# Turning h and the similarity's rows by transposing DMAs in a four-layer graph kernel, with four adjacency buffers

## Chip, cores and metric

One core of a Trainium2 chip. The metric is the device time of one execution in microseconds (us), median over runs.

## What is computed

Four pre-normalised graph layers with a residual each, on x (4096 x 256) and a dense adjacency A (4096 x 4096), all float32:

```python
h = relu(layernorm(x)); x = x + relu(An @ (A2 @ h @ W.T))         # A2 = A + I, An = d * A2 * d
h = relu(layernorm(x)); g = h @ Wg                                  # attention layer
x = x + softmax(cos(g, g) + log(A + 1e-8)) @ g + bias               # cos: rows of g scaled to length 1
h = relu(layernorm(x)); x = x + relu((dn * A * dn) @ h @ W2 + b2)   # dn from A's row sums
h = relu(layernorm(x)); t = relu([h, A @ h] @ W1)
x = x + relu([t, A @ t] @ W2')
```

## The kernel before, in words

**Passes.** The adjacency is gone through six times, passes 0 to 5: 0 and 1 are the first layer, 2 (`ATT`) is attention, 3 the third layer, 4 (`TURNED`, its result transposed) and 5 the fourth. A pass has 8 groups (`NG`) of 512 result rows, and a group has 8 chunks (`NC`) of 512 adjacency rows, 1 MB each. For float32 accuracy every operand is split into two float16 halves: ACT writes the upper half `ahi` of a chunk (`split`, L789), DVE the lower half `alo` (L1036), and PE multiplies upper by upper, upper by lower and lower by upper with the moving rows `mov` (`product`, L472 to L477; `product_turned`, L483 to L485). A chunk is 4 row blocks b of 4 products. Passes 1, 3 and 5 make a product from one 512-column and one 256-column matmul, passes 0 and 2 from three of 257, 256 and 257 columns, where the odd column gives row sums. `adj`, `ahi` and `alo` have two buffers each: SP loads chunk c when DVE has split chunk c-2 (`load`, L314), and ACT splits chunk c when PE has left chunk c-2 (`chunk_done`).

**The tail of a group.** While PE multiplies group g, the results of group g-1 go through stages: `ev` (out of PSUM), `epi`, `x` (residual), `stats` and `norm` of the layer norm, `h` (relu and its halves in `hsp`, ACT L868, DVE L1147), then the turn of h: PE transposes `hsp` block by block into `psT` (L547, stages T0 and T1, 8 transposes each), ACT copies it to `hT` (`keep_hT`, L879), and PE multiplies `hT` by the next weights (`small`, W0 and W1, 12 matmuls of 256 columns each, 24 in pass 3's tail, L592 to L594), whose result is split into `mov` (L901, L1171). In pass 1's tail the result is also scaled to unit rows (`n0`, `n1`: ACT L913, DVE L1185), turned by PE (`G0`, `G1`, `turn_gn`) and kept in `gnT` (L918) for the similarity (`cosines`, L701 to L703). Before pass 0 the same stages turn the first h (tail `PRE`).

**Order.** Each engine runs its own program in order, and tables by hand (`PLACES`, `ATT_PLACES`) say behind which chunk, and on PE behind which (chunk, block), each stage stands. PE: `(3, 3): T0, (4, 0): W0T1, (5, 0): W1, (6, 0): G0, (6, 2): G1` (L626). ACT: L946, DVE: L1218; there a stage at c stands behind split c. POOL (`tail`, L423) computes `own`, the group's own rows for the identity in A2 (L431, as soon as `mov` is there), and the powers -1/2 (`rstd` L417, `rowp`, `rnorm` L442). ACT's and SP's DMAs have a queue each; before the change ACT issues two, at the start.

Of the kernel before, what the change touches and what calls it, by code (L numbers as in the profile page):

```python
# [60 lines left out]

WARM = [60, 60]
# [9 lines left out]
def build(nc, x, adj_t, w0, wg, bias_g, w2, bias_2, w3a, w3b, sent, out):  # L72
# [4 lines left out]
    with ctx:  # L77
# [14 lines left out]
        gnT = shared[:, :].bitcast(f16).rearrange("p (q n) -> p q n", q=2 * FB)  # L92
# [54 lines left out]
        psT = pb("psT", [P, 2 * FB, 2 * P], f16)  # L147
# [3 lines left out]
        psT2 = psS[:, 0, :].bitcast(f16).rearrange("p (q n) -> p q n", q=2 * FB)  # L151
# [7 lines left out]
        adj_loaded = [sem(f"adj_loaded{s}") for s in range(2)]  # L159
# [42 lines left out]
        hT_ready = sem("hT_ready")  # L202
# [9 lines left out]
        gn_turned = sem("gn_turned")  # L212
        gnT_ready = sem("gnT_ready")
# [4 lines left out]
        NORM = [PRE, 1, 2, 3]  # L218
        SMALL = [PRE, 1, 2, 3, 4]
# [41 lines left out]
        def exp_slot_free(eng, g, H):  # L261

            g, H = (g, H - 4) if H >= 4 else (g - 1, H - 4 + NH)
            if g < 0:
                return
# [22 lines left out]
        def small_bank(p, b):  # L288

            if p == TURNED:  # L290
                return psW[:, :] if b % 2 == 0 else psS[:, 0, :]
            bank = psS[:, 0, :] if p == 3 else psS[:, 1, :] if p == PRE and b >= 2 else psW
            return bank[:, (b % 2) * F:(b % 2 + 1) * F]
# [5 lines left out]
        def _(sp):  # L299
# [36 lines left out]
            def group(p, g, first=False):  # L336
                for c in range(2 if first else 0, NC):
                    load(p, g, c)
# [16 lines left out]
            def att_half(g, H):  # L355

                c = H // 2
                if g == 0 and H < 4:
                    sp.wait_ge(split_ready, chunk_no(ATT - 1, NG - 1, NC - 2 + c) + 1)
# [44 lines left out]
        def _(pool):  # L404
# [18 lines left out]
            def tail(p, g):  # L423
                if p in SELF:
# [37 lines left out]
        def _(pe):  # L462
            def product(p, g, c, b, k, first, last):
# [10 lines left out]
                n = F + 1  # L474
# [47 lines left out]
            def turn(p, g, r):  # L522


                pe.wait_ge(h_ready, at(SMALL, p, g))

                if p == PRE:

                    if g > 0:
                        pe.wait_ge(hT_ready, at(SMALL, p, g - 1, 2, r + 1))  # L530
                elif r == 1:
                    pe.wait_ge(hT_ready, at(SMALL, p, g, 2, 1))
                elif not isinstance(g, int) or g > 0:
                    pe.wait_ge(hT_ready, at(SMALL, p, g - 1, 2, 2))
                    if p == 1:
                        pe.wait_ge(gnT_ready, at([1], p, g - 1, 2, 2))
                else:
                    before = SMALL[SMALL.index(p) - 1]
                    pe.wait_ge(hT_ready, at(SMALL, before, NG - 1, 2, 2))
                    if p == 2:  # L540
                        pe.wait_ge(gnT_ready, at([1], 1, NG - 1, 2, 2))
                transposes(r, work(p, g)[1], psT2 if p == PRE and r == 1 else psT).then_inc(h_turned, 1)

            def transposes(r, hsp, to):
                for q in range(2 * FB):
                    for b in range(2):
                        last = nc.tensor.transpose(to[:, q, b * P:(b + 1) * P],  # L547
                                                   hsp[:, q // FB, 2 * r + b, (q % FB) * P:(q % FB + 1) * P],
                                                   ident[:, :])
                return last  # L550

            def small(p, g, r):

                whi, wlo = weights_of[p]
                if p == TURNED:

                    pe.wait_ge(h_ready, at(SMALL, p, g))
                else:

                    pe.wait_ge(hT_ready, at(SMALL, p, g, 2, r + 1))  # L560

                if p == PRE:

                    if g > 0:
                        pe.wait_ge(mov_ready, at(MOVE, p, g - 1, GB, 2 * r + 2))
                elif r == 1:
                    pe.wait_ge(mov_ready, at(MOVE, p, g, GB, 2))
                    if p == 1:
# [789 lines left out]
```

## Time and profile before

| | |
|---|---|
| median of 3 runs | 2486.02 us (2483.68 to 2486.75) |
| span of the profiled execution, the only time that it has | 2484.0 us |
| busy: PE, PE's weight loads, DVE, ACT, POOL | 98%, 66%, 59%, 46%, 6% |
| DMA | 473 MB, 191 GB/s on average |
| passes, us from the start | 0: 82 (start before it), 1: 407, 2: 777, 3: 1370, 4: 1787, 5: 2140 |

An engine's busy time says how much of the span it had an instruction in work. Matmuls overlap in the pipe, so PE's true pace is read from one start to the next. A wait "PE acc L472 <- DVE alo L1036: 12.1, 8, 1.7" says that PE sat idle 12.1 us in 8 times, at most 1.7, until DVE's L1036 had written `alo`.

### The profile page before, as it was taken

Reading aid. Unit: us, or ns where it says so; the run is one execution under the profiler, and the core shown is the slowest. Engines: PE = TensorE matmul, PEld = TensorE weight load, DVE = VectorE, ACT = ScalarE, POOL = GpSimd, SP = SyncE. Lnnn points to the kernel's source line nnn. Section 1 sums busy time; section 2 is a strip of 40 time slices with the busy share of each in tenths; the row PEclk is TensorE's granted clock in tenths of the full one; section 3 lists DMA queues with packets and bytes.
Section 4 is the critical chain, followed back from the end, with each engine's and each line's share of the span. In section 5 each row is a group of like instructions: output and inputs, shape, how many; then the busy total and the mean of one; then the engine's idle time right before and its main releaser. Section 6 shows DMA issues by size and latency. Waiting matters only on the chain.

```text
span 2484.0 us, 43195 instructions
## 1 busy us (share of the span) xinstructions
PE 2434.0 (98%) x17096; PEld 1640.3 (66%) x17096; DVE 1462.1 (59%) x1899; ACT 1145.1 (46%) x1435; POOL 143.5 (6%) x114
## 2 busy tenths in 40 slices
PE   7999999999999999999999999999999999999999
PEld 6888887656666767777888666666544444555555
DVE  7655555666666566666777665566544444455555
ACT  6544443555555544444444444444434334343433
POOL 2300000111110000000000010001000000000000
PEclk9999999999999999999999999999999999999999
DMA  5455555545454766676676544444455455456564
GB/s 204 154 202 188 201 195 194 187 169 178 176 178 158 205 181 201 213 244 206 217 241 231 187 170 169 169 171 167 169 180 186 175 179 184 177 198 219 209 218 170
DMA packets 113727, 473.23 MB, mean 191 GB/s; under 512 B 14432, under 2 KB 47456, under 8 KB 72672
## 3 DMA queue, kind: packets, MB, share of 16 engines
q1 hardware_dynamic: 113344, 471.13, 55.5%
q8 instruction: 65, 1.06, 0.2%
q10 hardware_dynamic: 288, 0.79, 0.1%
q14 instruction: 30, 0.25, 0.0%
HBM read 438.32 MB, written 33.55 MB: 190 GB/s over the span
## 4 chain that ended last, share of the span: by engine, by line
issue 66%; PE 26%; POOL 5%; DMA 1%; DVE 1%; ACT 1%; POOLq 0%; SPq 0%; ACTq 0%; DVEq 0%
PE acc L472 8%; PE acc L483 4%; PE acc L485 4%; PE acc L484 4%; PE acc L473 4%; POOL rstd L417 3%; POOL own L431 1%; DMA adj<-in_adj_t 1%; DVE alo L1036 1%; ACT ahi L789 1%; PE psS L594 0%; PE psS L592 0%; PE psS L593 0%; POOL d L450 0%; PE psW L592 0%
## 5 line engine op out<-in xcount | busy, mean ns | idle before, releaser
L1036 DVE SCALAR_TENSOR_TENSOR alo<-adj,ahi 128x2048 f16<-128x2048 f32 x320 | 743.5, 2323 | 683.0 <-ACT ahi L789 683.0
L472 PE MATMUL acc<-mov,ahi 128*128 128x512 f16 x3072 | 1002.4, 379 | 26.4 <-DVE alo L1036 26.4
L789 ACT ACTIVATE ahi<-adj 128x2048 f16<-128x2048 f32 x320 | 610.9, 1909 | 716.9 <-PE acc L473 337.5
L473 PE MATMUL acc<-mov,alo 128*128 128x256 f16 x3072 | 837.3, 273 | 0.0
L475 PE MATMUL acc<-mov,ahi 128*128 128x257 f16 x2048 | 558.1, 273 | 4.3 <-DVE alo L1036 2.4
L476 PE MATMUL acc<-mov,ahi 128*128 128x256 f16 x2048 | 560.9, 274 | 0.0
L477 PE MATMUL acc<-mov,alo 128*128 128x257 f16 x2048 | 556.2, 272 | 0.0
L472 PEld LDWEIGHTS acc<-mov,ahi 128*128 128x128 f16 x3072 | 300.5, 98 | 386.6 <-DVE alo L1036 32.0
L473 PEld LDWEIGHTS acc<-mov,alo 128*128 128x128 f16 x3072 | 300.6, 98 | 34.5
L475 PEld LDWEIGHTS acc<-mov,ahi 128*128 128x128 f16 x2048 | 196.8, 96 | 46.2 <-DVE alo L1036 4.4
L476 PEld LDWEIGHTS acc<-mov,ahi 128*128 128x128 f16 x2048 | 197.9, 97 | 39.4
L477 PEld LDWEIGHTS acc<-mov,alo 128*128 128x128 f16 x2048 | 202.0, 99 | 26.6
L981 ACT ACTIVATE ahi<-nums 128x512 f16<-128x512 f32 x256 | 160.5, 627 | 100.0 <-DVE nums L1248 98.9
L483 PE MATMUL acc<-ahi,mov 128*128 128x512 f16 x512 | 194.1, 379 | 1.5 <-DVE alo L1036 1.5
L484 PE MATMUL acc<-alo,mov 128*128 128x512 f16 x512 | 194.0, 379 | 0.0
L485 PE MATMUL acc<-ahi,mov 128*128 128x512 f16 x512 | 194.0, 379 | 0.0
L1248 DVE SCALAR_TENSOR_TENSOR nums<-adj,expo 128x512 f32<-128x512 f32 (+2 forms) x144 | 93.1, 646 | 153.3 <-ACT expo L964 153.1
L964 ACT ACTIVATE expo<-psS 128x512 f32<-128x512 f32 (+2 forms) x144 | 81.0, 562 | 209.9 <-PE psS L703 185.0
L1255 DVE SCALAR_TENSOR_TENSOR alo<-nums,ahi 128x512 f16<-128x512 f32 x256 | 175.3, 685 | 0.1
L417 POOL TENSOR_TENSOR rstd<-vare,neghalf 128x4 f32<-128x4 f32 x32 | 77.3, 2414 | 1184.5 <-DVE vare L1126 1184.5
L1248 DVE SCALAR_TENSOR_TENSOR nums<-adj,psS 128x512 f32<-128x512 f32 (+2 forms) x136 | 86.7, 637 | 36.2 <-PE psS L688 22.3
L701 PE MATMUL psS<-shared 128*128 128x512 f16 (+3 forms) x288 | 103.5, 361 | 0.4 <-DVE nums L1248 0.4
(109 smaller groups left out, 1965.3 us busy)
## 6 DMA issues: line engine op xcount, KB each, us to landing
adj<-in_adj_t SPq DMA_DIRECT2D x320, 1024.0 KB, 4.8
adj<-in_adj_t SPq DMA_DIRECT2D x128, 512.0 KB, 4.8
sent<-expo SPq DMA_DIRECT2D x112, 256.0 KB, 2.8
expo<-sent SPq DMA_DIRECT2D x56, 512.0 KB, 5.1
xres<-in_x SPq DMA_DIRECT2D x7, 512.0 KB, 9.9
out<-xres SPq DMA_DIRECT2D x7, 512.0 KB, 6.5
xres<-in_x ACTq DMA_DIRECT2D x1, 512.0 KB, 3.3
shared<-in_w3a SPq DMA_DIRECT2D x1, 512.0 KB, 6.5
```

Of the source, the lines that this page charges most:

```text
L472: nc.tensor.matmul(acc[:, b, :].rearrange("p (s n) -> p s n", s=2), hi, both, start=first, stop=False)
L473: return nc.tensor.matmul(acc[:, b, 0:F], lo, m[:, jb, 0:F], start=False, stop=last)
L475: nc.tensor.matmul(acc[:, b, 0:n], hi, m[:, jb, 0:n], start=first, stop=False)
L476: nc.tensor.matmul(acc[:, b, 0:F], hi, m[:, jb, LO:LO + F], start=False, stop=False)
L477: return nc.tensor.matmul(acc[:, b, 0:n], lo, m[:, jb, 0:n], start=False, stop=last)
L483: nc.tensor.matmul(acc[:, f, :], hi, ahi[:, c % 2, k, :], start=first, stop=False)
L484: nc.tensor.matmul(acc[:, f, :], hi, alo[:, c % 2, k, :], start=False, stop=False)
L485: return nc.tensor.matmul(acc[:, f, :], lo, ahi[:, c % 2, k, :], start=False, stop=last)
L789: nc.scalar.activation(ahi[:, c % 2, :, :], adj[:, c % 2, :, :], ACT.Copy, scale=ADJ_SCALE)\
L1036: nc.vector.scalar_tensor_tensor(alo[:, c % 2, :, :].rearrange("p b n -> p (b n)"), adj[:, c % 2, :, :].rearrange("p b n -> p (b n)"), ADJ ...
L1248: last = nc.vector.scalar_tensor_tensor(nums[:, n % NUMS, cols], adj[:, (j // GB) % 2, j % GB, cols], ADJ_EPS, e[:, cols], ALU.add, ALU.mult)
L1255: nc.vector.scalar_tensor_tensor(alo[:, (j // GB) % 2, j % GB, :], nums[:, n % NUMS, :], P_SCALE, ahi[:, (j // GB) % 2, j % GB, :], ALU.mu ...
```

## The change

`hsp` and `hT` are laid out so that one `dma_start_transpose` on ACT's queue turns all of a group's h: 128 x 2048 float16 into 16 blocks of 128 x 128 (`turn_h`, stage T), and another its unit rows into `gnT` (`turn_gn`, stage G). PE's T and G stages, `keep_hT` outside the start, and `keep_gnT` go. PE waits for `hT_landed` in front of W0, and W0 and W1 stand together behind block 1 of chunk 5, with two PSUM banks between them (`psX` is what `psT` was). ACT and DVE have h behind split 4 (it was 3), ACT has T behind split 5, W0 and W1 behind 6, n0, n1 and G behind 7. The adjacency has a ring of four buffers outside attention, two of them in `expo`, each loaded when the chunk four earlier is split. POOL's `own` waits in addition until chunk 5 of its group is split. The 257-column matmuls of passes 0 and 2 take 258 columns. ACT's loop over groups is written out in passes 1 and 3. Work buffers of the start move from `expo` to `nums` and `ev`. The core of the diff:

```diff
         nums = sb("nums", [P, NUMS, GR], f32)
+        ring = [adj[:, i, :, :].rearrange("p b n -> p (b n)") for i in range(2)]\
+            + [expo[:, 2 * i:2 * i + 2, :].rearrange("p b n -> p (b n)") for i in range(2)]
...
-        hsp2 = expo[:, 1, :].bitcast(f16).rearrange("p (s b n) -> p s b n", s=2, b=GB)
+        hsp = sb("hsp", [P, GB, 2, F], f16)
+
+        o2 = nums[:, 0:2, :].rearrange("p b n -> p (b n)").rearrange("p (b n) -> p b n", b=GB)
+        hsp2 = ev[:, :, :].rearrange("p b n -> p (b n)")[:, 0:GB * F].bitcast(f16)\
+            .rearrange("p (b s n) -> p b s n", s=2, b=GB)
         own = sb("own", [P, GB, F], f32)
-        hT = sb("hT", [P, 2 * FB, GR], f16)
+        hT = sb("hT", [P, GB * 2 * FB, P], f16)
+        hTq = hT[:, :, :].rearrange("p (b q) n -> p q b n", q=2 * FB)
...
+            elif p == 3:
+                bank = psS[:, b // 2, :]
+            else:
+                bank = (psW[:, :], psX)[b // 2]
             return bank[:, (b % 2) * F:(b % 2 + 1) * F]
 
...
 
-                    q, h, e = (p, g, c - 2) if c >= 2 else ((p, g - 1, c + 6) if not isinstance(g, int) or g > 0
-                                                            else (p - 1, NG - 1, c + 6))
+                    q, h, e = (p, g, c - 4) if c >= 4 else ((p, g - 1, c + 4) if not isinstance(g, int) or g > 0
+                                                            else (p - 1, NG - 1, c + 4))
                     if q == ATT:
-                        sp.wait_ge(num_ready, h * NB + GB * (e + 1))
+
+                        sp.wait_ge(num_ready, h * NB + (GB * (c + 7) if c < 2 else GB * (c + 5)))
                     else:
                         sp.wait_ge(split_ready, chunk_no(q, h, e) + 1)
                 row = g * (NC * P) + c * P
-                sp.dma_start(adj[:, c % 2, :, :].rearrange("p b n -> p (b n)"), adj_t[bass.ds(row, P), :])\
-                    .then_inc(adj_loaded[c % 2], 16)
+                sp.dma_start(ring[c % 4], adj_t[bass.ds(row, P), :]).then_inc(adj_loaded[c % 4], 16)
...
@@ -427,6 +442,8 @@
                     pool.wait_ge(mov_ready, at(MOVE, p - 1, g, GB, GB))
                     if not (isinstance(g, int) and p == 0):
                         pool.wait_ge(sum_ready, at(SELF, p, g, 1, 0))
+
+                    pool.wait_ge(split_ready, chunk_no(p, g, OWN) + 1)
                     rows = mov[p % 2][:, bass.ds(g * GB, GB), :]
...
                     return nc.tensor.matmul(acc[:, b, 0:F], lo, m[:, jb, 0:F], start=False, stop=last)
-                n = F + 1
+                n = LO
                 nc.tensor.matmul(acc[:, b, 0:n], hi, m[:, jb, 0:n], start=first, stop=False)
                 nc.tensor.matmul(acc[:, b, 0:F], hi, m[:, jb, LO:LO + F], start=False, stop=False)
...
+
+                    pe.wait_ge(hT_kept, 2 * g + r + 1)
...
-                    pe.wait_ge(hT_ready, at(SMALL, p, g, 2, r + 1))
...
-            def turn_gn(p, g, r):
-
-                pe.wait_ge(gn_ready, at([1], p, g, GB, 2 * r + 2))
-
-                if r == 0:
-                    pe.wait_ge(hT_ready, at(SMALL, p, g, 2, 2))
-                else:
-                    pe.wait_ge(gnT_ready, at([1], p, g, 2, 1))
-                transposes(r, hsp, psT).then_inc(gn_turned, 1)
-
             def step(name, p, g):
-                if name == "T0":
...
-            PLACES = {(3, 3): "T0", (4, 0): "W0T1", (5, 0): "W1", (6, 0): "G0", (6, 2): "G1"}
+
+            PLACES = {(5, 1): "W0W1"}
...
-            ATT_PLACES = [{10: "T0", 12: "W0T1", 15: "W1", 18: "G0", 20: "G1"}, {19: "T0", 22: "W0T1", 26: "W1"}]
+            ATT_PLACES = [{14: "W0W1"}, {23: "W0W1"}]
...
+            def turn_h(p, g):
+
+                act.wait_ge(h_ready, at(SMALL, p, g))
 
                 if not isinstance(g, int) or g > 0:
-                    act.wait_ge(small_ready, at(SMALL, p, g - 1, 2, r + 1))
-                elif p > PRE:
-                    act.wait_ge(small_ready, at(SMALL, SMALL[SMALL.index(p) - 1], NG - 1, 2, r + 1))
-                nc.scalar.activation(hT[:, :, 2 * P * r:2 * P * (r + 1)],
-                                     (psT2 if p == PRE and r == 1 else psT)[:, :, :], ACT.Copy)\
-                    .then_inc(hT_ready, 1)
+                    act.wait_ge(small_ready, at(SMALL, p, g - 1, 2, 2))
+                else:
+                    act.wait_ge(small_ready, at(SMALL, SMALL[SMALL.index(p) - 1], NG - 1, 2, 2))
+                act.dma_start_transpose(hT[:, :, :], hsp[:, :, :, :].rearrange("p b s n -> p (b s n)"))\
+                    .then_inc(hT_landed, 16)
+
+            def turn_gn(g):
+
+                act.wait_ge(gn_ready, at([1], 1, g, GB, GB))
+                act.dma_start_transpose(gnT[:, bass.ds(g * GB * 2 * FB, GB * 2 * FB), :],
+                                        hsp[:, :, :, :].rearrange("p b s n -> p (b s n)")).then_inc(gnT_landed, 16)
 
             def small_out(p, b):
 
...
-
-            PLACES = {0: ["ev"], 3: ["h"], 4: ["T0"], 5: ["W0", "T1", "n0"], 6: ["W1", "n1"], 7: ["g0", "g1"]}
-            ATT_PLACES = [{2: ["ev"], 10: ["h"], 14: ["T0"], 16: ["W0", "T1"], 17: ["n0"], 19: ["W1"],
-                           20: ["n1"], 22: ["g0"], 24: ["g1"]},
-                          {2: ["ev"], 17: ["h"], 23: ["T0"], 26: ["W0", "T1"], 30: ["W1"]}]
+                elif p == 1 and name == "G":
+                    turn_gn(g)
+
+
+            PLACES = {0: ["ev"], 4: ["h"], 5: ["T"], 6: ["W0", "W1"], 7: ["n0", "n1", "G"]}
+            ATT_PLACES = [{2: ["ev"], 10: ["h"], 11: ["T"], 15: ["W0"], 16: ["W1"], 18: ["n0"], 19: ["n1"], 21: ["G"]},
+                          {2: ["ev"], 17: ["h"], 18: ["T"], 26: ["W0"], 27: ["W1"]}]
 
...
-                    with act.Fori(1, NG) as g:
-                        group(p, g, p, g - 1)
+                    if p in TURN:
+
+                        for g in range(1, NG):
+                            group(p, g, p, g - 1)
+                    else:
+                        with act.Fori(1, NG) as g:
+                            group(p, g, p, g - 1)
...
-            PLACES = {0: ["ev"], 1: ["epi"], 2: ["x", "stats"], 3: ["norm", "h"], 5: ["W0", "n0"], 6: ["W1", "n1"]}
-            ATT_PLACES = [{2: ["ev"], 4: ["epi"], 6: ["x"], 7: ["stats"], 9: ["norm"], 10: ["h"], 16: ["W0"], 17: ["n0"],
-                           19: ["W1"], 20: ["n1"]},
-                          {4: ["epi"], 8: ["x"], 11: ["stats"], 14: ["norm"], 17: ["h"], 26: ["W0"], 30: ["W1"]}]
+            PLACES = {0: ["ev"], 1: ["epi"], 2: ["x", "stats"], 3: ["norm"], 4: ["h"], 6: ["W0", "W1"], 7: ["n0", "n1"]}
+            ATT_PLACES = [{2: ["ev"], 4: ["epi"], 6: ["x"], 7: ["stats"], 9: ["norm"], 10: ["h"], 15: ["W0"], 16: ["W1"],
+                           18: ["n0"], 19: ["n1"]},
+                          {4: ["epi"], 8: ["x"], 11: ["stats"], 14: ["norm"], 17: ["h"], 26: ["W0"], 27: ["W1"]}]
```

## Rows read from the trace of the kernel before

**Rows 1.** The page, part 1: busy us, share of the span, instructions.
```profile
PE 2434.0 (98%) x17096; PEld 1640.3 (66%) x17096; DVE 1462.1 (59%) x1899; ACT 1145.1 (46%) x1435; POOL 143.5 (6%) x114
```

**Rows 2.** Stages view, L547 alone: stretch, PE, PEld, granted clock, DMA, GB/s.
```profile
82.00:2484.00 2402.00, 39.02 (x512) 33.93 (x512) 1.00 0.56 191
```

**Rows 3.** Timeline of PE, pass 1: start us, us, instruction [idle before it].
```profile
699.73 0.61 PE L547 MATMUL psT<-ident,hsp 128*128 128x128 f16 x8
701.99 0.39 PE L472 MATMUL acc<-mov,ahi 128*128 128x512 f16 x1 [1.65 <-DVE alo L1036]
...
703.30 0.27 PE L592 MATMUL psW<-wsp,hT 128*128 128x256 f16 x1
...
704.61 0.61 PE L547 MATMUL psT<-ident,hsp 128*128 128x128 f16 x8
705.06 0.38 PE L472 MATMUL acc<-mov,ahi 128*128 128x512 f16 x1
...
710.26 0.27 PE L592 MATMUL psW<-wsp,hT 128*128 128x256 f16 x1
```

**Rows 4.** Waits of PE in passes 0, 1, 3 (from 1375 to 1800), 5: us, times, longest.
```profile
PE acc L475 <- DVE alo L1036: 2.4, 6, 0.4
...
PE acc L472 <- DVE alo L1036: 12.1, 8, 1.7
...
PE acc L472 <- DVE alo L1036: 12.4, 8, 1.6
PE acc L483 <- DVE alo L1036: 1.5, 1, 1.5
...
PE acc L472 <- DVE alo L1036: 0.9, 3, 0.4
```

**Rows 5.** Timeline of ACT, pass 1, one group.
```profile
498.21 1.91 ACT L789 ACTIVATE ahi<-adj 128x2048 f16<-128x2048 f32 x1 [3.29 <-PE acc L473]
504.41 2.08 ACT L868 ACTIVATE hsp<-xres,shift,rstd 128x256 f16 x4 [4.29 <-POOL shift L420]
506.39 1.90 ACT L789 ACTIVATE ahi<-adj 128x2048 f16<-128x2048 f32 x1
```

**Rows 6.** Timeline of DVE, the same group.
```profile
500.65 2.28 DVE L1036 SCALAR_TENSOR_TENSOR alo<-adj,ahi 128x2048 f16<-128x2048 f32 x1
503.84 1.38 DVE L1133 TENSOR_SCALAR o<-xres,mv,rstd 128x256 f32 x4 [0.91 <-POOL rstd L417]
```

**Rows 7.** Timelines of DVE and of POOL, pass 0.
```profile
189.88 3.67 DVE L1036 SCALAR_TENSOR_TENSOR alo<-adj,ahi 128x2048 f16<-128x2048 f32 x1 [1.45 <-ACT ahi L789]
...
189.50 1.90 POOL L431 TENSOR_TENSOR own<-mov 128x1024 f32 x1
```

**Rows 8.** Timeline of ACT, pass 5: a split that waited for its load.
```profile
2297.87 1.91 ACT L789 ACTIVATE ahi<-adj 128x2048 f16<-128x2048 f32 x1 [4.56 <-DMA adj<-in_adj_t]
```

**Rows 9.** Timeline of PE, pass 0, the first and the 19th L475.
```profile
299.81 0.27 PE L475 MATMUL acc<-mov,ahi 128*128 128x257 f16 x1
...
305.78 0.27 PE L475 MATMUL acc<-mov,ahi 128*128 128x257 f16 x1
```

**Rows 10.** DMA issues by tile: count: issue's ns min/median/max.
```profile
L314 SPq DMA_DIRECT2D adj<-in_adj_t x320: 327/333/471, 4.5 to 2463.7; - x160
...
L331 SPq DMA_DIRECT2D diag<-in_adj_t x4: 438/612/5257, 28.9 to 35.4; - x4
```

**Rows 11.** Timelines of ACT and DVE, pass 1: stage n1.
```profile
475.27 0.84 ACT L913 ACTIVATE hsp<-psW,rnorm 128x256 f16<-128x256 f32 x2 [1.26 <-POOL rnorm L442]
...
476.14 0.88 DVE L1185 SCALAR_TENSOR_TENSOR hsp<-psW,rnorm,hsp 128x256 f16<-128x256 f32 x2 [1.16 <-ACT hsp L913]
```

**Rows 12.** Stages view, attention: stretch, us, busy of PE, PEld, DVE, ACT, POOL.
```profile
777.00:1370.00 593.00, 591.12 (x4754) 459.84 (x4752) 400.52 (x747) 282.64 (x528) 12.60 (x18) 1.00 0.68 213
```

**Rows 13.** The page, part 6: DMA issues, KB each, median us to landing.
```profile
adj<-in_adj_t SPq DMA_DIRECT2D x128, 512.0 KB, 4.8
...
diag<-in_adj_t SPq DMA_DIRECT2D x4, 4.0 KB, 7.1
```

More of the change, by code:

```diff
@@ L59 @@
 GN_SCALE = 64.0
+OWN = 5
 WARM = [60, 60]
@@ L158, in build @@
         x_loaded = [sem(f"x_loaded{q}") for q in range(NG)]
-        adj_loaded = [sem(f"adj_loaded{s}") for s in range(2)]
+        adj_loaded = [sem(f"adj_loaded{s}") for s in range(4)]
         half_loaded = [sem(f"half_loaded{q}") for q in range(4)]
@@ L201, in build @@
         h_turned = sem("h_turned")
-        hT_ready = sem("hT_ready")
+        hT_kept = sem("hT_kept")
+        hT_landed = sem("hT_landed")
         small_ready = sem("small_ready")
@@ L290, in small_bank @@
             if p == TURNED:
-                return psW[:, :] if b % 2 == 0 else psS[:, 0, :]
-            bank = psS[:, 0, :] if p == 3 else psS[:, 1, :] if p == PRE and b >= 2 else psW
+                return (psW[:, :], psX, psS[:, 0, :], psS[:, 1, :])[b]
+            if p == PRE:
+                bank = (psW[:, :], psS[:, 1, :])[b // 2]
+            elif p == 3:
+                bank = psS[:, b // 2, :]
+            else:
+                bank = (psW[:, :], psX)[b // 2]
             return bank[:, (b % 2) * F:(b % 2 + 1) * F]
@@ L337, in group @@
                 for c in range(2 if first else 0, NC):
-                    load(p, g, c)
+                    load(p, g, c, first=first and c < 4)
                     if first and c == 3:
@@ L520, in bank_free, with turn @@
                     pe.wait_ge(ev_ready, at(ALL, p, g - 1, GB, b + 1))
[L522 to L536, printed above, removed]
-                else:
[L538 to L544, printed above, removed]
+            def turn(g, r):
+                pe.wait_ge(h_ready, at(SMALL, PRE, g))
+                if g > 0:
+                    pe.wait_ge(hT_kept, 2 * (g - 1) + r + 1)
+                hsp, to = work(PRE, g)[1], psT2 if r == 1 else psT
                 for q in range(2 * FB):
                     for b in range(2):
-                        last = nc.tensor.transpose(to[:, q, b * P:(b + 1) * P],
-                                                   hsp[:, q // FB, 2 * r + b, (q % FB) * P:(q % FB + 1) * P],
+                        last = nc.tensor.transpose(to[:, b, q, :],
+                                                   hsp[:, 2 * r + b, q // FB, (q % FB) * P:(q % FB + 1) * P],
                                                    ident[:, :])
-                return last
+                last.then_inc(h_turned, 1)
             def small(p, g, r):
@@ L587, in small @@
                     whi, wlo = whi[:, :, F:2 * F], wlo[:, :, F:2 * F]
-                for b in range(2):
-                    rows = slice((2 * r + b) * P, (2 * r + b + 1) * P)
-                    to = small_bank(p, 2 * r + b)
+                for b in (2 * r, 2 * r + 1):
+                    to = small_bank(p, b)
                     for f in range(FB):
-                        nc.tensor.matmul(to, hT[:, f, rows], whi[:, f, :], start=f == 0, stop=False)
-                        nc.tensor.matmul(to, hT[:, f, rows], wlo[:, f, :], start=False, stop=False)
-                        last = nc.tensor.matmul(to, hT[:, FB + f, rows], whi[:, f, :], start=False,
-                                                stop=f == FB - 1)
+                        hi, lo = hTq[:, f, b, :], hTq[:, FB + f, b, :]
+                        nc.tensor.matmul(to, hi, whi[:, f, :], start=f == 0, stop=False)
+                        nc.tensor.matmul(to, hi, wlo[:, f, :], start=False, stop=False)
+                        last = nc.tensor.matmul(to, lo, whi[:, f, :], start=False, stop=f == FB - 1)
@@ L850, in hi_of_h @@
                     act.wait_ge(small_ready, at(SMALL, q, e, 2, 2))
-                    nc.scalar.activation(hT[:, 0:FB, :], oT, ACT.Relu).then_inc(h_hi, GB)
+                    for f in range(FB):
+                        nc.scalar.activation(hTq[:, f, :, :], oT[:, f, :].rearrange("p (b n) -> p b n", n=P), ACT.Relu)\
+                            .then_inc(h_hi, GB // FB)
                     return
@@ L999, in _ @@
             for q in range(NG):
-                for name in ["T0", "T1", "W0"]:
-                    stage(name, PRE, q)
+                keep_hT(q, 0)
+                keep_hT(q, 1)
+                stage("W0", PRE, q)
                 if q + 1 < NG:
```

152 lines of the change are left out of this document (73 added, 79 removed).

## The prediction

> **What bounds the kernel now.** Read the busy shares first: the tensor engine (PE) is busy 98% of a span of 2484.0 us [rows 1], at the full granted clock of 2.4 GHz [rows 2], so the table of waits and the pace of PE come next, and the slower engines only as far as they hold PE up. The profile's span is 2484.0 us and the median of the three runs 2486.02; I make the sum against the span and add 2.0 us at the end.
>
> PE's pace is read from start to start, since a matmul's modelled end overlaps the next one. In the stretch of pass 1 [rows 3], eight transposes take 704.61 to 705.06, 0.056 us each; twelve 256-column matmuls take 703.30 to 704.61, 0.109 each; sixteen products of a 512- and a 256-column matmul take 705.06 to 710.26, so a chunk of 16 takes 5.2 us. PE idles in few places [rows 4]. In pass 1 it waits 8 times for DVE's lower half `alo` (12.1 us), in pass 3 after its first group's start and at the start of pass 4 9 times (12.4 and 1.5 us). Rows 3 show one: the transposes of T0 end near 700.18, and the next chunk starts at 701.99.
>
> Why DVE is late there stands in [rows 5, 6]; let S_c be the moment when PE starts chunk c. ACT may split chunk c+1 only when PE leaves chunk c-1, that is at S_c; its split takes 1.90 us and DVE's 2.28, so the halves are there 4.2 us after S_c, where PE needs them after 5.2. **The slack is 1.0 us.** In the group shown S_2 is 498.21, so S_3 is 503.4. ACT's stage h stands before split 4 and waits 4.29 us for POOL's powers, runs 504.41 to 506.49, and split 4 starts at 506.39 instead of 503.4: 3.0 us late, of which the slack covers 1.0, the eight transposes 0.45.
>
> **The change part by part.**
>
> (a) *Transposes leave PE.* After the start there are 512 of them [rows 2]; 512 x 0.056 = **-28.8 us**, all on PE's path. The 128 of the start stay. ACT also loses its 64 copies out of psT, worth nothing by itself, as ACT is not the bound; it makes room for (f). The small matmuls stay as many; they now run together after block 1 of chunk 5, and chunk 5 becomes 5.2 + 24 x 0.109 = 7.8 us long. Their second half no longer waits for the first to be read, because it has a bank of its own.
>
> (b) *Stage h moves behind split 4.* ACT then splits 4 at 503.4, DVE does the norm (1.38 us, ready at 505.2) and its half 505.3 to 507.6, against S_4 = 508.6. h takes 505.3 to 507.4 on ACT, and DVE is free for its part from 507.6 to 510.5; split 5 is at 508.6 on ACT and 510.5 on DVE. So the stall at T0 goes: 7 in pass 1, 8 in pass 3, 1 in pass 4. Each is 1.65 us by the waits and 0.16 more from start to start. The eighth wait of pass 1 is another's (c): 12.1 - 7 x 1.65 = 0.6. So 11.5 + 13.9 = 25.4, and 25.4 + 16 x 0.16 = **-28.0 us**. Late next would be DVE's half of chunk 3, behind x and stats: it ends at 502.93 [rows 6], 0.5 us before S_3, as now.
>
> (c) *POOL's sum `own` waits for split 5.* Where it runs beside DVE's split, that split takes 3.67 us [rows 7] and not 2.28 [rows 6], and six waits of 0.4 us follow in pass 0, 2.4 in all, and one of 0.6 at the start of pass 1. With 0.16 each: 7 x 0.16 + 3.0 = **-4.1 us**. Moved to the 3 us that DVE is idle before split 6 it costs nothing; behind `own` on POOL wait the powers of rows and norms, which are due only in the next group. The six waits of pass 0 stand in [rows 4].
>
> (d) *Four adjacency buffers.* In pass 5 ACT waits for a chunk's DMA [rows 8], and three waits of PE follow, 0.9 us, 1.4 with their 0.16. A load issued four chunks ahead, 20 us, hides its landing of 4.8 us even behind a store: **-1.4 us**. The same DMAs move the same bytes; the loads themselves bring nothing elsewhere. At the start loads 2 and 3 no longer wait, so the weights and the diagonal follow sooner on SP's queue, behind all of x; taken as 0, within 1 us either way.
>
> (e) *257 columns become 258.* No row has 258. Between 299.81 and 305.78 there are 18 triples of 257, 256 and 257 columns [rows 9]: 0.3317 us each. Three even ones of 256 take 3 x 0.1092 = 0.3276 [rows 3]; with the four added columns at 2.4 GHz 0.3292. If the odd width costs the excess, 2048 x 2.5 ns = -5.1 us; if it stays, two columns more cost +1.7. I take **-5.1**, since all even widths seen keep the plain pace; ends -5.1 and +1.7.
>
> (f) *The transposing DMAs*, which the trace does not show. Each is 512 KB within SBUF in one instruction on ACT's queue, and has two prices.
>
> How long it holds ACT: a plain load holds its queue 0.33 us; the four diagonal loads, 1024 pieces of 4 bytes each, hold theirs 0.44 to 5.26 us [rows 10]. The ends are 0.3 and 5.3; I take 2.5, between them, because a transpose of 128 x 2048 elements is cut far finer than a load of 128 long rows, and far from single elements. For T, issued at S_4 + 1.9 = 510.5 after split 5, ACT has 3.3 us until S_5 and 1.0 of slack: 2.5 is free. T's own wait, for DVE's part of h, has only split 6 queued behind it, and is over by then. For G in pass 1 it is not. With S_5 = 0, S_7 is 13.0. ACT splits 7 at 7.8 to 9.7, n0 and n1 take 0.84 us each to 11.4, DVE's split ends at 12.0 and its two pairs of 0.88 at 13.8 [rows 11]. So G goes at 13.9, 0.9 after the next split could start; PE stalls 0.9 + hold - 1.0, here 2.4 us, for the 7 groups of pass 1 **+16.8 us** (0.3: +1.4; 5.3: +36). In attention PE is busy 591.1 of 593.0 us [rows 12] beside a stage h of 2.1 us on ACT, so 2.5 is taken as free there; at 5.3 it is up to 5.3 - 2.1 = 3.2 us in each of 9 places, 29.
>
> How long until it lands: T from 510.5, wanted by PE at (5, 1), S_5 + 2.6 = 516.4: a window of **5.9 us**. Nearest rows: 512 KB of adjacency in 4.8 us, the diagonal's 4 KB in 7.1 [rows 13]. I take 5 to 5.5, inside the window, cost 0. At 7.1, 1.2 us x 16 = +19. A transpose has 2048 runs of 256 bytes, twice the diagonal's pieces; priced so it lands after 14.2 us. The Trainium skill (Advanced Engine Details and Errata, X-Bar Transpose) says that these DMAs are as fast as regular ones; by that T costs nothing. Its VectorE: DVE Perf Modes, in the section on the three transpose paths, puts a 128x128 block at 1309 ns by DMA and 390 on TensorE, which speaks against this change; no row of this trace shows either, and PE's 0.056 us of pace is far below 390 ns.
>
> *Small edits.* In pass 4 the two halves of h are written in two instructions each instead of one, some tenths of a us behind split 4, in the slack: 0. ACT's written-out loops move no work: 0.
>
> **Sum:** -28.8 - 28.0 - 4.1 - 1.4 - 5.1 + 16.8 = -50.6; 2484.0 - 50.6 = 2433.4, and with 2.0 for the median **2435.4 us**.
>
> **Rivals.**
> 1. *The issue is as cheap as other DMAs'* (0.33 us): G costs 1.4, the time is 2435.4 - 15.4 = 2420.0. For it: no issue of a large transfer holds its queue over 0.5 us. Against: the pieces are many. 0.2.
> 2. *T lands a little late* (7.1 us), PE waiting in front of the small matmuls: 2435.4 + 19.2 = 2454.6. For it: loads fill half of the DMA engines' time [rows 2], and one starts 2.9 us ahead of T, another 2.3 behind it. 0.13.
> 3. *Slower.* The sixteen blocks of a transpose go through one after another at the price of small pieces, and PE waits for `hT_landed` at (5, 1) in passes 1, 3 and 4: at 14.2 us it is 8.3 x 16 = +133 us, 2568; the loops around it stay, so nothing makes up for it. It decides from where 16 (t - 5.9) eats the 50.6 us, t = 9.1 us. For it: the diagonal's 7.1 us for 4 KB; against: elements of 4 bytes are the worst case, runs here have 256. By the skill's 1309 ns, 16 blocks would take 20.9 us, and the time would be 2675. 0.1.
> 4. *The reorder frees nothing*, since DVE and not ACT's place is late: 2435.4 + 28.0 = 2463.4. Against: the wait stands behind ACT's late split [rows 5]. 0.04.
>
> My forecast has 0.53. **Range** 2414 to 2461: below, rival 1 with own slips of 6 us; above, rival 2 and the odd width kept (+6.8); outside lie rival 3 and half of rival 4, and holds near 5.3. A measurement of this kernel tells some 0.2% (5 us) from no change. Faster: forecast, rivals 1, 2 and 4, less a share for long holds and landings between 7 and 9 us, 0.87; same 0.02; slower 0.11.
>
> **What would show it.** PE's L547 count is 128. The waits for `alo` in pass 1 fall to the 7 at a group's start after G, some 2.4 us each, in pass 3 to none; a group of pass 3 without stall is 8 x 5.2 + 48 x 0.109 = 46.8 us. ACT's issue takes 2.5 us and lands within 5.9. L475 to L475 is 0.329. A PE wait on the landing in front of L592 would be rival 2 or 3; DVE splits of 2.3 us everywhere confirm (c).

## The result and the profile after

The changed kernel takes **2460.1 us** (median of 4 runs, 2456.4 to 2462.2) against 2485.3 of the kernel before (4 runs): a ratio of 0.990, 95% interval 0.988 to 0.991, 25 us faster. The forecast was 2435.4 us in a range of 2414 to 2461. Direction and range held, the range by 0.9 us: two of the four runs (2461.8 and 2462.2) lie above it. The gain was half of what the sum said. The profiled execution of the changed kernel, the fastest of the four, has a span of 2454.6 us.

Busy shares and queues on the page after (against [rows 1]; the third line is ACT's DMA queue, before 0.79 MB):

```profile
PE 2408.8 (98%) x16584; PEld 1614.4 (66%) x16584; DVE 1450.2 (59%) x1907; ACT 1082.2 (44%) x1379; POOL 143.7 (6%) x114
...
DMA packets 180289, 490.00 MB, mean 200 GB/s; under 512 B 80993, under 2 KB 114017, under 8 KB 139233
...
q10 hardware_dynamic: 66848, 17.57, 3.7%
```

PE has exactly 512 instructions fewer, and is as full as it was. So the lost gain must stand among PE's waits. The waits of PE after, in pass 1, in pass 3 with the start of pass 4, and in attention (against [rows 4]):

```profile
PE acc L489 <- DVE o L1043: 17.4, 6, 4.3
PE psW L590 <- DMA hT<-hsp: 1.9, 1, 1.9
...
PE psW L582 <- DMA hT<-hsp: 2.3, 1, 2.3
...
PE acc L492 <- DVE alo L1257: 2.9, 2, 2.2
PE acc L492 <- DVE o L1043: 1.4, 1, 1.4
PE psS L683 <- ACT expo L957: 0.7, 1, 0.7
PE psS L683 <- DVE nums L1250: 0.4, 1, 0.4
```

No wait for `alo` is left in passes 1, 3 and 4, where there were 16 at T0: the reorder did what it should. In their place, six waits in pass 1 end with DVE's L1043, the stage ev that clears a result bank, 17.4 us and up to 4.3 each; twice PE waits for `hT` to land; attention has five waits, of which the two of 1.4 and 0.4 us were there before.

The passes, from the first product of one to the first product of the next (to the last matmul for pass 5), in us, read from PE's timeline for the kernels that change a pass (the bounds of the passes ahead of the prediction are rougher, by up to 23 us):

```
kernel               start  pass 0  pass 1  pass 2  pass 3  pass 4  pass 5
before                22.2   375.2   383.5   590.6   393.0   375.6   339.7
the change            22.4   370.1   382.5   588.3   376.2   373.1   337.9
x1_order              22.3   371.7   382.8   590.6   379.3   374.0   339.5
x2_sp                 22.3   371.7   357.4   590.1   372.1   373.1   337.9
x7_gplace             22.4   370.1   363.4   592.1   374.1   373.1   337.9
x6_spall              22.2   371.7   357.4   585.8   372.1   373.1   337.9
x4_half               22.2   371.7   401.1   590.9   376.1   373.1   337.9
```

Pass 3 gave 16.8 us; pass 1, where the change takes away more transposes (224 against 128) and nearly as many stalls (7 against 8), gave 1.0, and attention 2.3. (Pass 0 differs by 1.6 us between kernels with the same code there: with 370.1 a dip of the clock in the first 40 us is missing. So 3.5 us of its 5.1 are the change's.)

**Where pass 1 lost it.** ACT's timeline after, at the end of a group of pass 1; ACTq is ACT's queue as it issues a DMA:

```profile
468.14 1.91 ACT L771 ACTIVATE ahi<-expo 128x2048 f16<-128x2048 f32 x1 [1.27 <-PE acc L490]
...
470.67 0.84 ACT L917 ACTIVATE hsp<-psT,rnorm 128x256 f16<-128x256 f32 x2
473.98 3.95 ACTq L883 DMA_TRANSPOSE shared<-hsp  x1
478.03 1.91 ACT L771 ACTIVATE ahi<-adj 128x2048 f16<-128x2048 f32 x1 [6.52 <-issue]
479.85 1.18 ACT L808 ACTIVATE o<-acc 128x256 f32<-128x256 f32 x4
```

G is issued at 473.98, once DVE's halves n0 and n1 are there, and the queue is held for 3.95 us. The split of the next chunk, which PE's progress would have allowed at 473.3 (5.2 us behind the one at 468.14), starts at 478.03. Behind it on DVE stand the lower half and then ev, on PE the bank that ev clears (timelines of DVE and PE, the same place):

```profile
479.97 2.29 DVE L1035 SCALAR_TENSOR_TENSOR alo<-adj,ahi 128x2048 f16<-128x2048 f32 x1 [6.03 <-ACT ahi L771]
482.18 1.41 DVE L1043 SCALAR_TENSOR_TENSOR o<-acc,o 128x256 f32<-128x256 f32 x4
```

```profile
478.17 0.27 PE L490 MATMUL acc<-mov,alo 128*128 128x256 f16 x1
482.66 0.39 PE L489 MATMUL acc<-mov,ahi 128*128 128x512 f16 x1 [4.21 <-DVE o L1043]
```

478.03 + 1.9 + 2.3 + 0.4 is 482.6; PE starts at 482.66, where it wanted bank 0 at 478.3: 4.4 us from start to start beyond the pace. And the stall has an echo. The stages view over the stretch before, in, behind and after it; the seventh column is the granted clock:

```profile
474.00:478.00 4.00, 4.00 (x27) 2.44 (x26) 0.00 (x0) 0.00 (x0) 0.00 (x0) 1.00 0.88 292
478.00:482.60 4.60, 0.44 (x4) 0.05 (x1) 2.63 (x3) 4.57 (x6) 0.00 (x0) 1.00 0.26 58
482.60:486.60 4.00, 3.94 (x14) 1.93 (x15) 4.00 (x5) 0.23 (x1) 0.00 (x0) 0.57 0.75 262
486.60:490.00 3.40, 3.40 (x23) 2.06 (x21) 1.46 (x5) 0.19 (x1) 0.00 (x0) 1.00 0.91 304
```

The clock is full before the stall, and in the 4 us behind it 0.57 on average, that is mostly at the lower level of 1.2 GHz; the matmuls at that level take twice their time. The 32 matmuls behind the three long stalls take 6.89, 6.76 and 6.49 us, where they take 5.21 behind a short one: 1.3 to 1.7 us more are lost, 1.5 on average. One group later the queue is held for only 1.33 us (ACT's timeline), and PE waits 1.6, from start to start 1.76, with no loss of clock:

```profile
524.26 1.33 ACTq L883 DMA_TRANSPOSE shared<-hsp  x1
525.70 1.91 ACT L771 ACTIVATE ahi<-adj 128x2048 f16<-128x2048 f32 x1 [3.91 <-issue]
```

```profile
530.33 0.39 PE L489 MATMUL acc<-mov,ahi 128*128 128x512 f16 x1 [1.60 <-DVE o L1043]
```

Three groups of the first and three of the second kind: 3 x (4.4 + 1.5) + 3 x 1.76 = 23.0 us. With the 2.0 of a late `hT` in the same pass that is 25.0, and pass 1 is 25.1 us shorter in x2_sp below, which has none of these waits.

### The profile page after: what moved, and what is told of

Read it like the earlier page. It is cut to its first block, busy times and chain, and to the rows that moved or that the text cites. A ratio compares the mean times of both kernels' runs of the same rounds, so it can differ in the third digit from the quotient of the medians.

```text
span 2454.6 us, 41678 instructions
## 1 busy us (share of the span) xinstructions
PE 2408.8 (98%) x16584; PEld 1614.4 (66%) x16584; DVE 1450.2 (59%) x1907; ACT 1082.2 (44%) x1379; POOL 143.7 (6%) x114
## 2 busy tenths in 40 slices
DMA packets 180289, 490.00 MB, mean 200 GB/s; under 512 B 80993, under 2 KB 114017, under 8 KB 139233
## 4 chain that ended last, share of the span: by engine, by line
PE 90%; issue 3%; DVE 2%; ACT 2%; ACTq 1%; POOL 1%; DMA 1%; DVEq 0%; POOLq 0%
PE acc L489 25%; PE acc L490 12%; PE acc L493 8%; PE acc L492 8%; PE acc L494 8%; PE acc L502 5%; PE acc L500 5%; PE acc L501 5%; PE psS L683 2%; PE psS L685 2%; PE psS L684 2%; PE psS L669 2%; ACT ahi L771 1%; POOL rstd L432 1%; DMA hT<-hsp 1%
## 5 line engine op out<-in xcount | busy, mean ns | idle before, releaser
L489 PE MATMUL acc<-mov,ahi 128*128 128x512 f16 x3072 | 1004.2, 380 | 18.2 <-DVE o L1043 17.4
L1035 DVE SCALAR_TENSOR_TENSOR alo<-expo,ahi 128x2048 f16<-128x2048 f32 x160 | 366.6, 2291 | 348.4 <-ACT ahi L771 348.4
L492 PE MATMUL acc<-mov,ahi 128*128 128x258 f16 x2048 | 558.4, 273 | 4.8 <-DVE alo L1257 2.9
L494 PE MATMUL acc<-mov,alo 128*128 128x258 f16 x2048 | 556.4, 272 | 0.0
L1035 DVE SCALAR_TENSOR_TENSOR alo<-adj,ahi 128x2048 f16<-128x2048 f32 x160 | 366.6, 2291 | 320.9 <-ACT ahi L771 318.8
L771 ACT ACTIVATE ahi<-expo 128x2048 f16<-128x2048 f32 x160 | 305.6, 1910 | 479.9 <-PE acc L490 297.5
L771 ACT ACTIVATE ahi<-adj 128x2048 f16<-128x2048 f32 x160 | 305.4, 1909 | 366.4 <-PE acc L490 178.4
L492 PEld LDWEIGHTS acc<-mov,ahi 128*128 128x128 f16 x2048 | 196.9, 96 | 46.0 <-DVE alo L1257 5.6
```

The lines of the kernel that those rows point to most:

```text
L489: nc.tensor.matmul(acc[:, b, :].rearrange("p (s n) -> p s n", s=2), hi, both, start=first, stop=False)
L492: nc.tensor.matmul(acc[:, b, 0:n], hi, m[:, jb, 0:n], start=first, stop=False)
L494: return nc.tensor.matmul(acc[:, b, 0:n], lo, m[:, jb, 0:n], start=False, stop=last)
L771: nc.scalar.activation(ahi[:, c % 2, :, :].rearrange("p b n -> p (b n)"), ring[c % 4], ACT.Copy, scale=ADJ_SCALE)\
L1035: nc.vector.scalar_tensor_tensor(alo[:, c % 2, :, :].rearrange("p b n -> p (b n)"), ring[c % 4], ADJ_SCALE, ahi[:, c % 2, :, :].rearrange( ...
```

## Experiments

Eight kernels; the comparison kernel for times is the one before, run on the same chip beside each. The diffs show the core of each edit: `...` stands for lines left out, and the comments in them are explanations, not code.

### x1_order: the reorder and the wait of `own` alone

```diff
+                    pool.wait_ge(split_ready, chunk_no(p, g, 5) + 1)   # before own
...
+            LATER = {(4, 1): "T0", (5, 0): "W0T1", (6, 0): "W1"}       # PE
+            LATER = {0: ["ev"], 4: ["h"], 5: ["T0"], 6: ["W0", "T1"], 7: ["W1"]}   # ACT, likewise on DVE
+                    for name in (LATER if tp in (2, 3, 4) else PLACES).get(c, []):
```

> The kernel before, with PE's transposes kept, and two parts of the change alone: POOL's own sum waits for split 5, and in the tails other than pass 1's the stages stand one chunk later (h behind split 4, T0 behind (4, 1), W0T1 behind (5, 0), W1 behind (6, 0)). Theory: in pass 3 the change's gain is the order's, not the DMAs'. Then pass 3, first product to first product of pass 4, falls from 393.0 to 377.7 us (nine stalls of 1.7 gone), against 376.2 with the whole change; pass 0 falls from 375.2 to 371.2, pass 4 from 375.6 to 374.0, passes 1, 2 and 5 stay (383.5, 590.6, 339.7), the whole is about 2464 us. Rival: the stall at T0 went because PE's transposes went; then pass 3 stays at 393 or its stall moves to the new place, and the whole is about 2480.

Measured: 2465.4 us, ratio 0.992 (0.990 to 0.994); pass 3 took 379.3 us, pass 0 371.7, pass 4 374.0. The waits of PE from the second group of pass 1 to the start of pass 5:

```profile
PE acc L473 <- DVE alo L1041: 12.6, 8, 1.8
PE acc L476 <- DVE o L1049: 1.5, 1, 1.5
PE psS L704 <- DVE nums L1255: 0.4, 1, 0.4
```

Of pass 3's 16.8 us, 13.7 come from the order alone, with PE still transposing; the rest of the change, in this pass the transposing DMAs, adds 3.1 to that in the changed kernel and 7.2 where none lands late (x2_sp, 372.1), which is what the pass's 128 transposes on PE take, 128 x 0.056 = 7.2 us. The eight waits left are pass 1's seven, where I had kept the old places, and one at the start of pass 3. So some 20 us, where the change gave 25, needed no transposing DMA (2485.3 to 2465.4). Pass 0's 3.5 us are the wait of `own` alone.

### x2_sp: the transposing DMAs on SP's queue, outside attention

```diff
...
+                    if turns and c == 0:
+                        turn_h(*turns)          # the same waits, sp.dma_start_transpose
+                    if turns and c == 3 and turns[0] == 1:
+                        turn_gn(turns[1])
...
-            PLACES = {0: ["ev"], 4: ["h"], 5: ["T"], 6: ["W0", "W1"], 7: ["n0", "n1", "G"]}
+            PLACES = {0: ["ev"], 4: ["h"], 6: ["W0", "W1"], 7: ["n0", "n1"]}
```

> The changed kernel with the transposing DMAs outside attention issued from SP's queue instead of ACT's (T behind SP's load 0, G behind its load 3). Theory: the stalls of pass 1 come from ACT's queue being held 4 us by G, 0.9 us after it should have split the next chunk. Then pass 1 falls from 382.5 to about 356 us (three stalls of 4.4 with the slow clock behind them, three of 1.8 and one of 2.0 gone), pass 3 keeps its one late landing or loses it (376 to 372), and the whole is 2430 to 2436 us. SP's queue shows the holds. Rival: pass 1's tail is too long for its places, or the transposes' traffic delays the loads, whoever issues them: pass 1 stays within 5 us of 382.5 and the whole above 2450.

Measured: **2430.5 us**, ratio 0.977 (0.976 to 0.979); pass 1 took 357.4 us, 25.1 less than with the change, as expected to 1.4 us. SP's timeline at the same G, and ACT's beside it:

```profile
475.56 3.82 SPq L365 DMA_TRANSPOSE shared<-hsp  x1
479.43 0.58 SPq L330 DMA_DIRECT2D adj<-in_adj_t  x1
```

```profile
474.93 1.91 ACT L805 ACTIVATE ahi<-adj 128x2048 f16<-128x2048 f32 x1 [1.83 <-PE acc L524]
```

SP is held as long as ACT was, but what stands behind it is a load that is wanted some 20 us later. ACT splits at 474.93, when PE lets it. PE has no wait at all in pass 1 up to the similarity's first product. That excludes the rival that the traffic itself is the cost: the bytes are the same, each transpose is issued at the same point of PE's work, and the loads in flight beside it were issued 0.7 to 1.6 us ahead of it in both kernels.

Attention took 590.1 us, 1.8 more than in the change, though its transposes were left as there. The wait of 1.45 us at its start, which every kernel has, is followed here by a stretch at the lower clock and was not before (stages view of x2_sp, then of the kernel before, over the 4 us behind that wait):

```profile
751.50:755.50 4.00, 4.00 (x17) 2.28 (x18) 2.10 (x6) 0.09 (x1) 0.00 (x0) 0.57 0.42 145
```

```profile
781.00:785.00 4.00, 4.00 (x31) 2.88 (x30) 2.57 (x7) 1.12 (x2) 0.00 (x0) 1.00 0.45 141
```

The same 32 matmuls take 6.04 us in the one and 4.37 in the other. So the length of a stall alone does not tell whether the clock falls behind it.

### x7_gplace: ACT's queue kept, G one group later behind split 1

```diff
+                    if tp == 1 and c == 1 and tg > 0:
+                        turn_gn(tg - 1)
...
-            PLACES = {0: ["ev"], 4: ["h"], 5: ["T"], 6: ["W0", "W1"], 7: ["n0", "n1", "G"]}
+            PLACES = {0: ["ev"], 4: ["h"], 5: ["T"], 6: ["W0", "W1"], 7: ["n0", "n1"]}
```

> The changed kernel, all transposing DMAs on ACT's queue as there, but G one group later, behind split 1 (in attention behind j = 3 for the last but one), where ACT has 3.3 us of idle time and 1.0 us of slack. Theory: only the place of G costs; held 4.0 us from S_1 - 3.3, ACT is 0.7 us late for split 2, within the slack. Pass 1 falls from 382.5 to 357 to 360 us (357.4 with SP's queue), the whole is about 2435. Rival: the traffic of a transpose beside a load is what PE waits for; then pass 1 stays over 375.

Measured: 2435.7 us, ratio 0.980 (0.978 to 0.981), as expected in total, though pass 1 took 363.4 us and not 357 to 360. The waits of PE in pass 1:

```profile
PE psW L590 <- DMA hT<-hsp: 5.4, 3, 2.2
```

The six waits for ev are gone though G holds ACT as long as ever: it was the place. The 6 us over x2_sp are three landings of `hT`, 8.8 to 9.5 us after their issue instead of the usual 6.3. On ACT's queue such late ones occur in the change too (two), in the passes outside attention of x2_sp none: there T lands within 5.6 to 6.8 us of its issue. The one in pass 1's last group is late in all three traces that issue it whole from ACT (8.8 to 9.1 us: the change, x3_lo, x7_gplace) and in none of the four that issue it from SP (6.5 to 6.6), so the queue has a part in it. The load that SP issues 4.2 us behind T does not tell the cases apart: it lands 8.9 to 10.1 us behind T's issue where T is late, and 9.1 to 9.6 in the change where T is not. How the two queues' transfers mix on the DMA engines was not tried by itself; the cause stays open.

### x6_spall: attention's transposes on SP's queue too

```diff
+                            if H == (11 if g else 8):
+                                turn_h(*((ATT, g - 1) if g else (1, NG - 1)))
+                            if (g, H) == (0, 13):
+                                turn_gn(NG - 1)
```

> The kernel with the transposes on SP's queue (x2_sp), now those of attention too: h's behind half load 11 of a group (8 in the first), G behind 13. Theory: attention gained 2.3 us and not 8.1 because ACT is held 1.3 to 4.2 us at T, which PE feels as waits for alo and expo (6 us with the slow clock behind the longest). Then attention falls from 590 to about 584 us and the whole to 2424. Rival: SP is the busier queue there; held, it sends and fetches the exponentials late, PE waits for the fetched ones, and attention rises above 592.

Measured: **2425.9 us**, ratio 0.976 (0.974 to 0.977), the fastest kernel of the study; attention took 585.8 us against 590.1. In the changed kernel the longest wait there came from T's hold (ACT's timeline in attention, after):

```profile
1327.33 3.81 ACTq L877 DMA_TRANSPOSE hT<-hsp  x1
1331.52 1.15 ACT L974 ACTIVATE ahi<-nums 128x512 f16<-128x512 f32 x2 [5.03 <-issue]
```

ACT stands for 5.0 us between two splits of numerators, and PE waits 2.2 us for `alo` behind it, with a loss of clock again. In x6_spall that stall and its loss of clock are gone. The lower clock at attention's start is still there, and so is a wait of 0.7 us for `expo`, which therefore was not the hold's.

### x4_half: each transpose in two DMAs of 8 blocks

```diff
+                for r in range(2):
+                    act.dma_start_transpose(hT[:, 8 * r:8 * r + 8, :],
+                                            hsp[:, 2 * r:2 * r + 2, :, :].rearrange("p b s n -> p (b s n)"))\
+                        .then_inc(hT_landed, 16)
```

> The changed kernel with each transposing DMA split into two of 8 blocks. With 16 blocks ACT's queue is held about 4.2 us in three of four and 1.33 in every fourth, whatever loads fly beside it. Theory: the queue's room for entries sets the hold, so that the sum over two halves keeps the pattern (three stages of 3.5 to 4.5 us, a fourth of about 2.7). Rival: the hold follows the blocks: each half takes 2.1 us, with no stage that is short. A third: the hold comes from loads in flight beside it; then the pattern follows the loads and not the count. The time stays within 10 us of 2460.

Measured: one run of 2479.0 us, 19 us over the changed kernel, more than any of the three theories allowed; pass 1 took 401.1. The issues, as count and ns min/median/max, in the changed kernel, with halves, and with SP's queue:

```profile
L877 ACTq DMA_TRANSPOSE hT<-hsp x24: 1333/4214/4687, 455.3 to 1760.6; - x24
...
L883 ACTq DMA_TRANSPOSE shared<-hsp x8: 1332/1672/4007, 474.0 to 826.0; - x8
```

```profile
L878 ACTq DMA_TRANSPOSE hT<-hsp x48: 1247/1352/3584, 456.8 to 1784.5; - x48
...
L886 ACTq DMA_TRANSPOSE shared<-hsp x16: 1247/1354/2742, 475.5 to 849.2; - x16
```

```profile
L359 SPq DMA_TRANSPOSE hT<-hsp x16: 3934/4254/4777, 456.9 to 1734.9; - x16
...
L365 SPq DMA_TRANSPOSE shared<-hsp x7: 1696/3746/3966, 475.6 to 740.9; - x7
```

With halves the first takes 1.25 to 1.5 us and the second 2.3 to 3.6 beside a load, 1.4 with little traffic; the sum of a G is 3.5 to 3.9 us in each of six groups, so each of them has a long stall (4.0 to 4.4 us) and the clock's echo, here 1.5 to 2.8 us. With two late landings that is the 43.7 us of pass 1 over x2_sp. The short hold of every fourth transpose on ACT's queue (1.33 us for the 4th, 8th, 12th, 20th, 28th and 32nd, 1.5 for the 16th and 2.2 to 2.5 for the 24th, in the change, in x3_lo and in x7_gplace alike) appears neither with halves nor on SP's queue. So it is no property of the blocks, and the theory of a queue's room for entries, as I put it, failed too. What is clear is the part of the traffic: on SP's queue the only G with no other DMA in flight, at 740.88, held 1.70 us; those beside a 1 MB load 3.55 to 3.97. In x6_spall the eight T of attention, issued from SP with next to nothing else in flight, held 1.70 to 1.94. Why every fourth 16-block transpose on ACT's queue is short stays open.

### x3_lo, x5_triple, x8_even: the 3.6 ns in the triple of passes 0 and 2

```diff
-LO = F + 2
+LO = F + 4                                   # x3_lo, n stays F + 2
...
+                nc.tensor.matmul(acc[:, b, 0:n], lo, m[:, jb, 0:n], start=False, stop=False)             # x5_triple:
+                return nc.tensor.matmul(acc[:, b, 0:F], hi, m[:, jb, LO:LO + F], start=False, stop=last) # this one last
...
+                nc.tensor.matmul(acc[:, b, 0:n], hi, m[:, jb, LO:LO + n], start=False, stop=False)       # x8_even
```

> The changed kernel with the lower halves of mov starting at column 260 instead of 258 (an 8-byte boundary in every row, instead of a 4-byte one); the width 258 is kept. The triple of matmuls takes 331.5 ns with 257 and with 258 columns, 3.5 ns over the pace of even widths, and the excess stands behind the middle matmul, the one that reads the lower halves. Theory: it is that start's alignment; then the pace behind it falls from 112.8 to 109.2 ns, the triple to 327.9, and the time by 2048 x 3.6 ns = 7.4 us to 2452.7. Rival: it has to do with the narrower result in the bank or with the change of weights; then the triple stays at 331.5 and the time at 2460.

> x2_sp with the triple's order changed: upper by upper (258 columns), lower by upper (258), then upper by lower (256). Neither the odd width nor the start of the lower halves carries the 3.6 ns behind the second matmul. Theory: the excess belongs to loading alo as weights; then it stands behind the first matmul now (109.6 to about 113), the triple stays at 331.5 and the time at 2430. Rival: it belongs to the narrow matmul in the middle of wider ones; now narrow is last, and the excess stands before the next triple or vanishes: 328 and 2423 us.

> x6_spall with the middle matmul of the triple also 258 columns wide (the two columns behind the lower halves are set to 0). The 3.6 ns excess moved with that matmul when it was put last, and did not go with an 8-byte start. Theory: it comes from its result being narrower than its neighbours' in the same bank; then all three take the plain 109.9 ns, the triple 329.7 instead of 331.5, and the time falls by 2048 x 1.8 = 3.6 us to 2422. Rival: it comes from where the lower halves lie; then the triple is 332.3 and the time 2427.5.

x5_triple is built on x2_sp (2430.5 us) and x8_even on x6_spall (2425.9), the other two on the change. Measured, with the mean distance in ns from each of the three matmuls to the next, over some 1765 triples of each trace:

```
kernel      order (hi = upper, lo = lower)    to the 2nd  to the 3rd  to the next  triple   us
before      hi.hi 257, hi.lo 256, lo.hi 257     109.6       112.7       109.2       331.5   2485.3
the change  hi.hi 258, hi.lo 256, lo.hi 258     109.6       112.8       109.2       331.5   2460.1
x3_lo       the same, lower halves at 260       109.3       112.8       109.2       331.3   2456.1
x5_triple   hi.hi 258, lo.hi 258, hi.lo 256     110.3       109.3       112.7       332.2   2430.0
x8_even     all 258                             109.5       113.6       109.2       332.2   2427.5
```

PE's timeline of the changed kernel, two L492 18 triples apart (against [rows 9], 5.97 us apart):

```profile
299.67 0.27 PE L492 MATMUL acc<-mov,ahi 128*128 128x258 f16 x1
...
305.64 0.27 PE L492 MATMUL acc<-mov,ahi 128*128 128x258 f16 x1
```

5.97 us again. The excess is behind the matmul that reads the lower halves, wherever that stands and however wide it is; an odd width, the 8-byte start, the weights and the narrower result are excluded as its cause. x3_lo's 4 us less in total is not the triple's: it lies within the spread of its runs (2454.3 to 2466.5), and in its trace no landing of pass 3 was late, where in the change's one was. x8_even's rival held, with 2427.5 us as it said; x5_triple took the time of its theory, but its triple fits neither of its two. The cause stays open.

## Why the prediction was right, and where it failed

The range held, and the mechanism of the gain was the one given; the time came out 24.7 us over the forecast. By its own steps:

(a) **Transposes leave PE**: right. PE has 512 instructions fewer, and in x2_sp pass 3 is 7.2 us shorter than with PE's transposes in the same order, 7.2 by count.

(b) **The stall at T0 goes**: right, all 16, and x1_order shows 13.7 us of it in pass 3 with no DMA involved. Rival 4 is refuted.

(c) **`own`**: right; 3.5 us in pass 0 and 0.7 in pass 1 of x1_order, against 4.1 for both.

(d) **Four buffers**: right; pass 5 fell by 1.8 us (1.4 said) in every kernel that has them, and not in x1_order (0.2).

(e) **258 columns**: wrong, 0 instead of -5.1. I took the excess of the triple for the odd widths', because no other triple was on record, and did not look behind which of the three it stood: it was the even one.

(f) **G's price**: the step that failed most, in the slack and in a term that the sum did not have. That the queue is held was right. G went 0.6 us after the time at which ACT could have split (473.98 against 473.3), where 0.9 was said. The hold was 4.0 us in three groups and 1.3 in three, 2.65 on average: close to the 2.5 taken between two far ends, and by luck, since neither kind is near it. But the slack was 0.3 us, not 1.0. I had counted it to the end of DVE's split, while the first thing that PE waits for at a group's start is the bank cleared by ev, another 0.4 us behind the split; and I had taken ACT's start of a split for PE's start of the chunk, which lies 0.26 us earlier (473.08). So even the short hold costs 1.76 us and the long one 4.4, and behind the long ones the lower clock takes 1.5 us more, which the sum had no term for. That is 23.0 us in six groups instead of 16.8 in seven (G of the seventh is issued where ACT has nothing due). Rival 1 leaned on a misreading as well: in the trace before, one 512 KB load of weights (L325) held its queue for 0.68 us.

**T's window** was wider than said. I let T go when split 5 has ended; ACT issues it as soon as h is there, 0.2 us after split 5 begins (the change, ACT's timeline):

```profile
455.12 1.91 ACT L771 ACTIVATE ahi<-adj 128x2048 f16<-128x2048 f32 x1 [1.32 <-PE acc L490]
455.32 4.33 ACTq L877 DMA_TRANSPOSE hT<-hsp  x1
```

PE's place behind (5, 1), in PE's timeline of the same group:

```profile
462.66 0.27 PE L590 MATMUL psW<-wsp,hT 128*128 128x256 f16 x1
```

From 455.32 to 462.66 are 7.3 us and not 5.9. T landed after 6.3 us, later than the 5.0 to 5.5 taken, and was in time by the one error that offset the other, which is luck: in a window of 5.9 us all sixteen would have been late. Two of sixteen came late (9.1 and 9.6 us) and cost 2.0 and 4.1 us, the second with the clock: rival 2 in part. Rival 3, block by block at the price of small pieces, did not happen: no T of the changed kernel outside attention took longer than 9.7 us, where 14.2 or 20.9 were needed. The Trainium skill's "as fast as regular DMAs" (Advanced Engine Details and Errata, X-Bar Transpose) fits the lone transpose and not those beside a load: a transpose of 512 KB took 6.3 us beside loads and 4.3 alone, where regular loads took 4.9 (512 KB) and 4.8 (1 MB). The Trainium skill's 1.3 us for one block (VectorE: DVE Perf Modes, the three transpose paths) does not multiply: sixteen blocks in one DMA took 6.3 us, 0.39 each.

**Attention**: taken as free, the transposing DMAs cost 6 of the 8 us that PE's transposes gave back. I compared the hold with a stage h of 2.1 us, but ACT was held for 3.8 us at worst, and a chain of numerators stood behind it. That one stall and its echo are 4.0 us of the six, and x6_spall shows that they were the queue's.

Added up: 6.2 (G) + 6.1 (late landings) + 5.8 (attention) + 5.1 (258 columns) = 23.2 us, less the 1.6 of the clock's dip that is missing in pass 0 and the 0.4 by which pass 5 did better than said: 21.2, which is the distance from the forecast's span of 2433.4 to 2454.6. The other 3.5 of the 24.7 us lie between the profiled execution and the median of the runs, and no trace tells them.

## What to carry to other kernels

A DMA transpose is free for the tensor engine, not for the queue that issues it: give it to the engine whose next instruction has the most slack (here SP, with loads four chunks ahead: 60 us of gain instead of 25, x6_spall against the kernel before beside it). Count the slack of a stage made late to the first thing that its consumer waits for, through every engine in the chain, and allow for what the clock may take back behind a stall. And try the reorder alone before the new mechanism: here it brought most of what the change as written gained.

## What the runs showed of the hardware

- A DMA transpose of 128 x 2048 float16 within SBUF holds its queue 1.7 to 1.9 us with nothing else in flight (x2_sp at 740.88, the change at 764.32) and 3.5 to 5.1 beside a 1 MB load, on ACT's and on SP's queue, but for every fourth on ACT's (mostly 1.33 us, unexplained); a plain load of 1 MB holds it 0.33 (median). Each moves 0.5 MB in pieces under 512 bytes: the page counts 80,993 such packets after and 14,432 before.
- PE stalls of 4.4 us were followed by a stretch at the lower clock that cost 1.3 to 1.7 us more, and so were two of 2.3 to 2.4 us in the changed kernel (at 1330.5 and 1435.9, 1.7 us each). One of 2.4 us in x7_gplace (at 551.0) was not, nor were those of 1.8 and 2.0 us in the change. One of 1.45 us idle was, in x2_sp and x6_spall (1.7 us), and not in the kernel before, the change, x1_order and x7_gplace. What decides it, beside the length, is open.
- The matmul that reads the lower halves of `mov` in passes 0 and 2 is followed by its successor 3.5 to 4.1 ns late, whatever its place or width.
